# First outputs kept in SBUF between a global attention and six local layers, with their norms taken during the attention and the first layer's weights in four parts on two queues

## The reference, cut to what matters

```python
x = L0_attn_hidden_states                       # (1, 2048, 128)
x = x + attn(layernorm(x), ...)                 # global attention: this sum is called x1 in the kernel
x = x + ffn(layernorm(x), ...)                  # six local layers; layernorm(x1) is what they begin with
# ffn:
for i in range(6):
    x = attn_layer(shift_tokens(x), Wqkv[i], q_scale[i], k_scale[i], Wo[i]) + x
    x = ffn_layer(shift_tokens(x), ln_g[i], ln_b[i], W1[i], b1[i], W2[i], b2[i]) + x
```

## Time and profile before

| | us |
|---|---|
| runs | 3246.62, 3246.05, 3249.65 (median 3246.62) |
| the profiled execution, its own time | 3259.23 |
| its span in the trace | 3257.4 |
| global attention, from the start to the last projected block | 0 to 1474 |
| from there to the first projection of the local layers | 1474 to 1502 |
| local layers | 1502 to 3257 |

### The profile page before, as it was taken

The page is one execution under the profiler, slowest core; times in us unless marked ns, Lnnn a source line. Parts: engine busy times, 40 slices in busy tenths (PEclk is TensorE's granted clock), DMA queues, the critical chain, the costliest instruction groups (busy, mean ns, idle before and its releaser), DMA issues.

```text
span 3257.4 us, 122555 instructions
## 1 busy us (share of the span) xinstructions
PE 2989.6 (92%) x53463; PEld 2278.3 (70%) x53463; DVE 2433.3 (75%) x3495; ACT 2033.3 (62%) x2669; POOL 2283.7 (70%) x1528
## 2 busy tenths in 40 slices
PE   4389999999999999994999999999999999999998
PEld 2267777777777777772677777777777777777776
DVE  4777777777777777734878778787877878787775
ACT  2345555555555555552677777777777777777775
POOL 1635555555555454306999999999999999999995
PEclk8589999999999999997999999999999999999999
DMA  5544445444444444404322233223223322322221
GB/s 116 101 80 86 77 84 88 85 79 86 81 83 84 78 84 84 84 5 124 82 64 63 69 79 83 59 68 96 66 67 81 83 58 69 94 68 67 68 76 45
DMA packets 253990, 251.90 MB, mean 77 GB/s; under 512 B 81999, under 2 KB 198624, under 8 KB 253328
## 3 DMA queue, kind: packets, MB, share of 16 engines
q1 hardware_dynamic: 251776, 243.67, 35.4%
q10 hardware_dynamic: 1680, 0.40, 0.1%
HBM read 96.22 MB, written 40.37 MB: 42 GB/s over the span
## 4 chain that ended last, share of the span: by engine, by line
PE 38%; ACT 8%; issue 4%; DVE 1%; POOL 1%; SPq 0%; DMA 0%; ACTq 0%; DVEq 0%; POOLq 0%
PE R L1235 11%; PE R L1242 10%; PE R L1345 5%; PE R L1259 5%; PE R L1333 4%; ACT kT L1364 3%; ACT sq L1376 3%; ACT kT L1369 2%; PE psB L1314 2%; PE R L1255 1%; PE psA L1308 0%; DVE mx L1513 0%; DVE ssq L1538 0%; DVE k L1504 0%; DMA xs_f<-xm 0%
## 5 line engine op out<-in xcount | busy, mean ns | idle before, releaser
L660 ACT ACTIVATE prob<-psS 128x1024 f32<-128x1024 f32 x512 | 524.0, 1024 | 598.7 <-PE psS L537 591.2
L824 DVE TENSOR_TENSOR colmax<-psS,colmax 128x1024 f32<-128x1024 f32 x480 | 587.3, 1224 | 309.1 <-PE psS L537 307.9
L537 PE MATMUL psS<-diag,pst 128*128 128x64 bf16 x16384 | 585.9, 195 | 26.6 <-issue 26.4
L1235 PE MATMUL R<-wqkv,xsT 128*128 128x512 f32 x1152 | 573.2, 620 | 37.1 <-ACT sq L1376 31.3
L537 PEld LDWEIGHTS psS<-diag,pst 128*128 128x128 f16 x16384 | 519.1, 99 | 87.3 <-issue 33.9
L529 PE MATMUL psS<-qst,kst 48*128 48x128 bf16 (+1 forms) x8192 | 382.0, 221 | 125.6 <-DMA pst<-p_parts 89.9
L758 POOL TENSOR_TENSOR rel<-rel,rec 128x1024 f32<-128x1024 f32 x64 | 151.7, 2370 | 484.7 <-DVE rec L837 484.7
L1364 ACT ACTIVATE kT<-R 64x1024 f32<-64x1024 f32 x192 | 195.7, 1019 | 423.7 <-PE R L1242 422.6
L529 PEld LDWEIGHTS psS<-qst,kst 48*128 48x128 bf16 (+1 forms) x8192 | 236.1, 95 | 282.4 <-issue 173.0
L1235 PEld LDWEIGHTS R<-wqkv,xsT 128*128 128x128 f32 x1152 | 196.9, 190 | 227.4 <-issue 159.6
L571 PE MATMUL psO<-prob,v 128*9 128x128 f32 x8192 | 326.6, 275 | 12.6 <-issue 11.3
(11 more groups left out here) (190 smaller groups left out, 6076.2 us busy)
## 6 DMA issues: line engine op xcount, KB each, us to landing
v<-vs SPq DMA_DIRECT2D x576, 128.0 KB, 2.4
pst<-p_parts SPq DMA_DIRECT2D x512, 128.0 KB, 4.9
p_parts<-stage SPq DMA_DIRECT2D x64, 512.0 KB, 3.0
v<-vs SPq DMA_DIRECT2D x384, 64.0 KB, 2.0
wqkv<-in_L_ffn_Wqkv SPq DMA_DIRECT2D x18, 512.0 KB
q_stack<-qpart SPq DMA_DIRECT2D x6, 512.0 KB
qst<-q_stack SPq DMA_DIRECT2D x32, 96.0 KB, 5.4
wo<-in_L_ffn_Wo SPq DMA_DIRECT2D x6, 512.0 KB
```

What stands on the lines that cost most here:

```text
L537: last = pe.matmul(o, pst[:, par, g, P * jb:P * (jb + 1)], diag[:, par, g, h0:h0 + HH // 2, :], start=False, stop=(g == NG - 1), skip_grou ...
L660: act.activation(prob[:, st % 2, :], psS[:, slot_of("b", st)].rearrange("p a b -> p (a b)"), ACT.Exp)\
L824: dve.tensor_tensor(dst, src, dst, ALU.max).then_inc(a_read, 1)
L1235: last = pe.matmul(R[slot[kind, n]][:, c, :], xsT[:, n % 3, :], w[:, INNER * which + 512 * c:INNER * which + 512 * (c + 1)], start=True, s ...
```

## The change

The residual tile of the attention and the tile `xm` of the local layers become one tile, held over both stages, and so do the identity, the means and variances `mv16`, the inverse roots `rs16` and the semaphore `x1_dma`. The sum of line 897 is written in place. Behind it DVE takes this block's statistics, and POOL adds the epsilon and takes the inverse root (`root`) in a later eighth of its loop; for the last block both happen in the local pipeline (`bn15`, `ln15`). The store to HBM stays, since the last layer reads `x1` there, but nothing waits for it until step 4 of the local layers.

The block between the stages is gone. Its zero fills are divided between POOL (`half1`, `vs`, `v2`) and DVE (`xsT`, `zeros`, `kT`), and at the head of the local block DVE norms blocks 0 and 1; the others follow one in a step. The first layer's loads are four parts with a semaphore each: SP issues part 0 (the q projection's weights and the six scale rows), the tables of blocks 0 and 1, and part 3 (13 loads); ACT issues parts 1 and 2 (the k and the v projection's weights), the masks and the tables of blocks 2 to 15. PE and POOL wait for the part that they need. Later layers have their 22 loads dealt to three parts in another way.

```diff
@@ attention, DVE, read_m("proj") @@
-                    dve.tensor_tensor(x1[:], psM[:, 0:D], xr, ALU.add).then_inc(m_read, 1)
+                    dve.tensor_tensor(x_res[:, blk, :], psM[:, 0:D], x_res[:, blk, :], ALU.add).then_inc(m_read, 1)
+                    if blk < NB - 1:
+                        dve.wait_ge(m_read, n + 1)
+                        if blk > 0:
+                            dve.wait_ge(ln_done, blk)
+                        dve.bn_stats(bn1[:], x_res[:, blk, :]).then_inc(ln_st, 1)
+                        dve.wait_ge(ln_st, blk + 1)
+                        dve.bn_aggr(mv16[:, blk, :], bn1[:]).then_inc(ln_done, 1)
@@ attention, POOL @@
+            def root(blk):
+                pool.wait_ge(ln_done, blk + 1)
+                pool.tensor_scalar(mv16[:, blk, 1:2], mv16[:, blk, 1:2], 1e-5, None, ALU.add).then_inc(ln_root, 1)
+                pool.wait_ge(ln_root, 2 * blk + 2)
+                pool.tensor_tensor(rs16[:, blk:blk + 1], mv16[:, blk, 1:2], minus_half[:], ALU.pow).then_inc(ln_root, 1)
...
+                    if k % 4 == 1 and not (first and k == 1):
+                        root(it * 2 + k // 4 - 1)
@@ attention, SP, the end @@
-            sp.wait_ge(x1_dma, 16 * NB)
@@ local_layers, load @@
+            first = [wqkv_part(0), *scales]
+            rest = [...]            # w2, b2, w1, ln_g, ln_b, wo, biases
+            jobs = (first, [wqkv_part(1), *rest[0:3], *biases[0:3]], [wqkv_part(2), *rest[3:7], *biases[3:6]]) if l else \
+                (first, [wqkv_part(1)], [wqkv_part(2)], rest)
...
+                    sp.dma_start(dst, src).then_inc(m["w_dma"] if l else w0_dma[part], 16)
@@ local_layers, the block between: removed whole (lines 1168 to 1206) @@
@@ local_layers, PE @@
+                        weights_here(pe, n, 0)      # q; the same with 1 before k, 2 before v, 3 before wo
...
+                            pe.wait_ge(m["xa_ready"], n + 1)
@@ local_layers, ACT, before its steps @@
+                load(act, 0, (1, 2))
+                act.dma_start(mask32[:], io["mask"]).then_inc(m["mask_dma"], 16)
+                act.dma_start(rope[:, 2:NB, :], io["rope"][:, 2:NB, :]).then_inc(rope_dma[1], 16)
@@ local_layers, POOL, before its steps @@
+                pool.memset(half1[:], -0.5).then_inc(m["ln15"], 1)
+                pool.memset(vs[:], 0.0).then_inc(m["zero_v"], 1)
+                pool.memset(v2[:], 0.0).then_inc(m["zero_v"], 1)
@@ local_layers, POOL, before the table of unit n @@
+                        weights_here(pool, n, 0)
+                        if n == 0 or n == 2:
+                            pool.wait_ge(rope_dma[n // 2], 16)
@@ local_layers, DVE @@
+                def normed(b):
+                    dve.tensor_scalar(xa[:, b, :], xm[:, b + 1, :], mv16[:, b, 0:1], rs16[:, b:b + 1], ALU.subtract, ALU.mult)\
+                       .then_inc(m["xa_ready"], 1)
+                dve.memset(xsT[:], 0.0).then_inc(m["zero_kT"], 1)
+                dve.memset(zeros[:], 0.0).then_inc(m["zero_kT"], 1)
+                normed(0)
+                normed(1)
+                dve.memset(xm[:, 0, :], 0.0)
+                dve.memset(kT[:], 0.0).then_inc(m["zero_kT"], 1)
+                dve.tensor_copy(identb[:], ident[:])
+                dve.wait_ge(m["mask_dma"], 16)
+                dve.tensor_copy(mask[:], mask32[:]).then_inc(m["masks_ready"], 1)
                 for s in STEPS:
+                    n = s + 2
+                    if s >= 0 and n < NB:
+                        if n == NB - 1:
+                            dve.wait_ge(m["ln15"], 5)
+                        normed(n)
@@ local_layers, SP, before its steps @@
+                load(sp, 0, (0,))
+                sp.dma_start(rope[:, 0:2, :], io["rope"][:, 0:2, :]).then_inc(rope_dma[0], 16)
+                load(sp, 0, (3,))
```

More of the change, by code:

```diff
@@ L415, in attention @@
         headsT = sb("headsT", [P, D])
-        x1 = sb("x1_sb", [P, D])
+        mv16, rs16, x1_dma = keep["mv16"], keep["rs16"], keep["x1_dma"]
+        bn1 = sb("bn1", [P, 6])
+        minus_half = sb("minus_half", [P, 1])
         psS = ctx.enter_context(nc.psum_tensor("psS", [P, 3, 2, 512], F32))
@@ L1125, in local_layers @@
         m = {n: sem(n) for n in names}
+        w0_dma = [sem(f"w0_dma{i}") for i in range(4)]
+        rope_dma = [sem(f"rope_dma{i}") for i in range(2)]
         v2_dma = [sem("v2_dma0"), sem("v2_dma1")]
@@ L1211, in local_layers, with weights_here @@
+                    sp.dma_start(dst, src).then_inc(m["w_dma"] if l else w0_dma[part], 16)
+        def weights_here(eng, n, part):
+            l = n // NB
+            if n % NB == 0:
+                if l:
+                    eng.wait_ge(m["w_dma"], l * (16 * NWL))
+                else:
+                    eng.wait_ge(w0_dma[part], 16 * (7, 1, 1, NWL - 9)[part])
         RING = (("S", 2), ("Q", 0), ("kT", 1), ("K", 0), ("V", 0), ("qT", 1), ("pT", 2), ("oT", 3), ("h", 5), ("O", 2))
@@ L1360, in _ @@
                             act.wait_ge(m["s_done"], n)
+                        else:
+                            act.wait_ge(m["zero_kT"], 3)
                         keys = flat[slot["kT", n]].rearrange("p (a b) -> p a b", b=P)
@@ L1487, in _ @@
                     if has(n):
+                        if n == 0:
+                            pool.wait_ge(m["ln15"], 3)
+                            pool.tensor_scalar(mv16[:, NB - 1, 1:2], mv16[:, NB - 1, 1:2], 1e-5, None, ALU.add)\
+                                .then_inc(m["ln15"], 1)
+                            pool.wait_ge(m["ln15"], 4)
+                            pool.tensor_tensor(rs16[:, NB - 1:NB], mv16[:, NB - 1, 1:2], half1[:, 0:1], ALU.pow)\
+                                .then_inc(m["ln15"], 1)
                         pool.wait_ge(m["lnv_done"], n + 1)
@@ L1636, in _ @@
                         sp.wait_ge(m["v_ready"], n + 1)
+                        if n == 0:
+                            sp.wait_ge(m["zero_v"], 2)
                         if n > 1:
@@ L1702, in program @@
     }
-    with ExitStack() as ctx:
-        global_attention(nc, ctx, io)
-    local_layers(nc, io)
+    with ExitStack() as outer:
+        sb = lambda n, s, d=F32: outer.enter_context(nc.sbuf_tensor(n, s, d))
+        shared = {"xm": sb("xm", [P, NB + 1, D]), "ident": sb("ident", [P, P]), "mv16": sb("mv16", [P, NB, 2]),
+                  "rs16": sb("rs16", [P, NB]), "x1_dma": outer.enter_context(nc.semaphore("x1_dma"))}
+        with ExitStack() as ctx:
+            global_attention(nc, ctx, io, shared)
+        local_layers(nc, io, shared)
 _INS = [f"L0_attn_{n}" for n in ("hidden_states", "Wq", "bq", "Wk", "bk", "Wv", "bv", "Wo", "bo", "rel_W", "rel_b",
```

110 lines of the change are left out of this document (37 added, 73 removed).

## The result

The change made the kernel slower. Five runs of the changed kernel took 3253.33, 3269.47, 3271.78, 3264.48 and 3254.19 us (median 3264.48), five of the kernel before 3244.93 to 3254.77 (median 3246.62): a ratio of 1.0041, 95% interval 1.0022 to 1.0061. Forecast were 19.4 us off; it came out some 13 us on top (0.0041 x 3246.62), or 17.9 from median to median.

What follows compares the result with a forecast made beforehand. PE, busy 92% of the span, bounds the attention; between the stages a 32.6 us chain of single steps runs alone. Gain 20.6 - 0.75 - 0.4 = 19.4 us, from 3246.62 to 3227.2, range 3221 to 3237.

Steps and rivals of the forecast that it cites:

- E: Rival, attention: DVE's late maximum costs PE a whole step of 2.29 us in each of 15 blocks; 3260.8 us; chance 0.04.
- Changeover: Between the stages: the first rotation moves from 1506.21 to 1485.6, a gain of 20.6 us.
- scale rows at 1481.8: Head of the local block: six scale rows, 0.1 MB, issued by 1477.6, land at 1481.8, near the lower bound 1479.7.
- upper bound: Scale rows at 1487.5 if 3.5 MB must pass first, 11.2 us; rotation then at 1491.3, a gain of 14.9.
- Rival B: Changeover: scale rows come late because ACT's big loads mix with them; gain 13.7 us, so 3232.9; chance 0.18.
- Statistics: Attention: the reciprocal starts 0.55 us later in 15 blocks, mostly absorbed; 0.05 each, 0.75 us in all.
- Rival C: Attention pays in full: each projected block delays PE by the whole 0.55 us, 8.2 in all; 3234.6; chance 0.12.
- POOL's product waits with slack behind it: Attention: the late reciprocal costs POOL's product nothing, as PE did not wait for the relation table in that stretch.
- POOL could be held by DVE: Local block's head: norms and casts could hold POOL's zero fills some 1 us; table at 1485.0, still ahead of 1485.6.
- Local steps: Local layers: 13 norms of 0.35 us at the head of DVE's steps, mostly absorbed by a wait; 0.4 us in all.
- In both stages alike, so I carry the difference over: Base: the profiled execution's 12.6 us above the median lay in both stages alike, so the gain was subtracted from 3246.62.
- PE as busy as before: Test in the profile after: PE in the stretch 300 to 1300 as busy as before, where it had 943 us.

Runs made afterwards that it cites:

- run 5: Kernel before with one unused tile of 192 bytes ahead of the attention's tiles, no instruction changed: 3273.7 us, 1.0074 of the kernel before.
- run 9: Kernel before, no instruction changed, with unused tiles of 160 and 480 bytes putting pst and stage on multiples of 512 bytes: 3220.45 us, 0.9922.
- run 1: The changed kernel again without any edit, in five more rounds: 3263.4 us, 1.0041 of the kernel before.
- run 6: Changed kernel with 64 unused bytes ahead of the attention's tiles, restoring their old placement modulo 256: 3246.82 us, 0.9983 of the kernel before.
- run 8: Changed kernel with unused tiles putting both pst and stage on multiples of 512 bytes: 3219.9 us, 0.9906 of the kernel before.
- run 2: Changed kernel with the tables of blocks 2 to 15 moved from ACT's queue to SP's: 3266.23 us, 1.0044 of the kernel before.
- run 3: Kernel before plus the attention's part alone (sum in place, statistics and roots, results unused), block between the stages kept: 3274.63 us, 1.0077.
- run 7: Kernel before plus the attention's part of the change alone, with 64 more bytes restoring the old placement: 3248.51 us, 0.9999.
- run 14: Changed kernel with pst and stage aligned, statistics and roots moved from the attention to the local block's head: 3213.08 us, 0.9902 of the kernel before.
- run 16: Aligned changed kernel with scale rows and first tables loaded early and statistics at the local block's head, blocks 0 and 1 first: 3208.41 us, 0.9857.

## Why the prediction was wrong

**The failed step: the tile that became one.** The change makes the residual tile and `xm` one tile. The prediction treated that as a matter of copies and waits, and counted nothing for where the other tiles then lie. They moved by 704 bytes, 192 modulo 256, and a move by 192 costs 24 us with the old instructions (run 5: 0.0074 x 3251). Less the 11 that the change gives at that place (below), this is the 13 us by which it came out slower. The time of the kernel before was no neutral base either: 0.8% of it is an accident of placement (run 9). None of the rivals had this mechanism; E had the sign and the size, with another cause.

With the attention's tiles at the same offset the change gains 0 to 11 us:

| `pst` offset | kernel before | changed | change alone, by the ratios |
|---|---|---|---|
| 32 | run 5, 1.0074 | run 1, 1.0041 | -11 us (within 8) |
| 96 | 1 | run 6, 0.9983 | -5.5 us (within 4) |
| 0 | run 9, 0.9922 | run 8, 0.9906 | -5 us (within 6); -0.6 by the medians, 3220.45 and 3219.9 |

Runs 5 and 1, and runs 9 and 8, are of different groups, so these two rows are rough. The traces of runs 9 and 8, whose spans differ by 0.1 us, show where the forecast's gain went there: the changeover gave 11.7 us (32.3 to 20.6), the attention took back 7.7 (1157.1 to 1164.8) and the local layers 4.8 (1751.9 to 1756.7).

The rest of the sum, term by term:

- **Changeover, forecast 20.6, measured 12.0.** Entering the local block, the transpose and POOL's fills went as worked out: fill `v` ended 10.0 us behind the last sum's start (forecast 9.7), the transpose began 3.1 behind it (forecast 2.0, the first norm took 1.48 and not 0.35). What failed is "scale rows at 1481.8", 8.2 us behind the last sum: PE was let go 16.8 behind it. That is beyond the upper bound too (13.9). The bound was taken from bytes, 3.5 MB at 0.31 MB per us; pieces of 128 to 256 bytes do not go by bytes. Rival B named the right victim and, in the main, the wrong cause: without ACT's tables it is 14.8 (run 2). The weights themselves took 5.2 us from issue, 0.1 more than worked out (1.7 + 3.4).
- **Statistics, forecast 0.75.** The chain worked out for it holds: in run 8 the reciprocal starts 0.75 us behind the sum's start, and PE does not wait longer for DVE's maximum (from 300 to 1430 in all 14.1 us in 35 waits, 13.9 in 35 in run 9). Rival C's mechanism is refuted. They cost nothing measurable at the offsets 32 and 96 (run 3 against run 5: 1.0077 and 1.0074; run 7: 0.9999), and some 9 us when aligned (run 14). "POOL's product waits with slack behind it" was where the working stopped: that product comes later, and DVE is held beside it.
- **POOL and DVE.** The prediction weighed that POOL could be held by DVE. It is DVE that is held: the first norm took 1.48 us (it ended at 1483.44, POOL's `vs` fill at 1483.36) where the later ones take 0.34, and the cast of the identity 1.54, ending at 1490.45 with POOL's `v` fill (1490.37). The rule cited there (the Trainium skill, GPSIMD Engine Reference, Key points) names DVE operations in a two-port mode or with two SBUF inputs as those in contention; the guard's operation has two, and this trace agrees with it. The norm and the cast have one each and were held too; in which mode they ran the trace does not show. Where no POOL operation ran beside it, the same cast took 0.16 us (the kernel before, run 14).
- **Local steps, forecast 0.4.** The norms cost nothing in a typical step: it takes 17.83 or 17.84 us in all kernels. But from the first rotation to the end the five traces with the old local part took 1751.2 to 1755.5 us (median 1751.9), and the 13 with the changed one 1750.5 to 1759.2 (median 1755.2). So this part lost some 3 us. It lies behind the last rotation (to the end 69.7 us in the median, 65.7 with the old part). In every changed kernel nearly all of the local layers' tiles lie 192 bytes further on too, modulo 256, and no pad moved these. Whether the loss is theirs or that of the new instructions no run shows.
- **The base.** "In both stages alike, so I carry the difference over" treated 12.6 us of one execution as noise without a place. Sum to sum, the attention took 1189.7 us in it, and 1182.3 and 1178.1 in runs 6 and 7 at the same offset, so most of it lies there.

Expectations of "PE as busy as before" in the stretch 300 to 1300 were the test that could have told: 940 against 943 looked like it held, and hid an execution picked from the lucky end. Sum to sum in repeated executions shows it better.

Open: why PE's instruction pages arrive late in just these places; why the offset 32 is worse than 64 to 160; the local layers' 3 us; what makes the scale rows late without the tables beside them.

## What to carry to other kernels

Before an edit that adds, merges or removes a tile is timed, look at where the built program puts the tiles that DMAs land in, before and after; put the busy ones on 256-byte boundaries in both, and only then compare. Otherwise an idle pad can decide the sign of the result. Load short rows long before they are asked for: what they take is not their bytes. And an engine's operation that is free by the count of its own cycles can still be paid where it moves a neighbour beside another engine's long operation.

## What the runs showed of the hardware

- The landing address in SBUF changes the time of a 1024-byte DMA row: 97.3 to 99.6 ns on a 256-byte boundary, 109.2 to 118.0 ns off it (80.4 to 82.0 and 89.2 to 94.3 with the stores counted in). With that go 25 to 50 us of this kernel. The address from which a store is taken changes its row by little: 46.2 to 48.6 ns.
- A DVE operation of 0.16 to 0.34 us that begins beside a POOL operation can last until that one ends: 1.15, 1.48 and 1.54 us, and 5.65 us in run 16. It does not always: from 300 to 1400 in run 8, 457 DVE operations began while one of POOL's ran, and ten of them were held so, five each of lines 885 and 889, each ending within 0.06 us of a POOL operation; in runs 9 and 14 none was.
- Six scale rows, 0.1 MB in pieces of 128 to 256 bytes, took 11.7 us to land beside other loads, and 9.6 with the tables behind them on the same queue (run 2). The DMA queues of the changed kernel from 1490 to 1494 show that about as many of ACT's large rows (q10) were moved as of SP's short ones (q1), whatever their size:

```profile
q10 hardware_dynamic: 123, 1.72, 100.7%
...
q1 hardware_dynamic: 140, 0.02, 3.2%
```
